# Softplus in the first stage of a one-core layer chain: the rounding rest used as it is, the bias as a ninth product row, maximum and subtraction in one VectorE operation

## The reference, cut to what matters

```
x_dbl = einsum('ble,er->blr', u2, W_xp)
dt_lo, Bm, Cm = x_dbl[..., :8], x_dbl[..., 8:24], x_dbl[..., 24:]
dt = softplus(einsum('blr,re->ble', dt_lo, W_dt) + b_dt)
A = -exp(A_log)
# for each step t:
dA = exp(dt_t[..., None] * A)
h  = dA * h + (dt_t * u_t)[..., None] * Bm_t[:, None, :]
y_t = einsum('ben,bn->be', h, Cm_t)
```

## Time and profile before

| | |
|---|---|
| median of 3 runs | 1540.54 us (1540.09 to 1544.02) |
| span of the profiled execution, its own time | 1563.6 us |
| busy, share of the span: PE, DVE, ACT, POOL | 80%, 65%, 51%, 44% |
| mean granted TensorE clock | 0.902 |
| first work of the four `dt` tiles to the first scan | 35.55 us to 73.71 us |
| loop of the first stage, POOL from first to last product | 73.87 us to 264.13 us |

### The profile page before, as it was taken

One profiled execution on the slowest core, in us unless ns is written; L12 is line 12 of the kernel. 1 busy time (PEld: TensorE's weight loads), 2 busy tenths in 40 slices (PEclk: granted clock), 3 DMA queues, 4 the chain that ended last, 5 costly groups with the idle time before them and its releaser, 6 DMA issues.

```text
span 1563.6 us, 27322 instructions
## 1 busy us (share of the span) xinstructions
PE 1245.3 (80%) x10088; PEld 884.4 (57%) x10088; DVE 1019.5 (65%) x1934; ACT 793.7 (51%) x1635; POOL 694.3 (44%) x688
## 2 busy tenths in 40 slices
PE   6788988224775667878878669988998999986996
PEld 2477877213453324444457424455776777875996
DVE  6898988751111988888663544457976785643774
ACT  4788686102333347767842325546665555321442
POOL 1199987574665430000023310025870881044553
PEclk9689999556888769999989789999999999987998
DMA  6378692112232432211001232111000003001113
GB/s 224 133 279 305 216 365 79 42 48 66 80 84 78 167 104 62 65 59 37 10 27 30 84 128 66 39 57 42 1 1 1 1 1 162 1 26 50 48 46 99
DMA packets 75508, 133.48 MB, mean 85 GB/s; under 512 B 12771, under 2 KB 39846, under 8 KB 74736
## 3 DMA queue, kind: packets, MB, share of 16 engines
q1 hardware_dynamic: 66448, 115.45, 22.0%
q0 software_dynamic: 8064, 13.87, 2.8%
q10 hardware_dynamic: 864, 2.43, 0.4%
HBM read 95.70 MB, written 38.38 MB: 86 GB/s over the span
## 4 chain that ended last, share of the span: by engine, by line
PE 49%; issue 19%; DVE 12%; ACT 8%; DMA 3%; SPq 3%; POOL 3%; another core or an unknown queue 2%; DVEq 0%; POOLq 0%; ACTq 0%
PE ps L1958 5%; PE ps L4214 3%; DVE sb_arena L2024 3%; PE ps L2325 2%; PE ps L718 2%; ACT sb_arena L2272 2%; POOL sb_arena L1116 2%; PE ps L2308 2%; PE ps L2575 1%; PE ps L3295 1%; PE ps L676 1%; PE ps L4181 1%; PE ps L4182 1%; PE ps L4183 1%
## 5 line engine op out<-in xcount | busy, mean ns | idle before, releaser
L2024 DVE TENSOR_REDUCE sb_arena<-ps 128x2 f32<-128x1024 f32 (+2 forms) x192 | 211.2, 1131 | 54.1 <-PE ps L2561 32.5
L2272 ACT ACTIVATE sb_arena<-ps 128x512 f32<-128x512 f32 (+1 forms) x320 | 160.3, 554 | 52.3 <-PE ps L2325 48.4
L921 DVE TENSOR_TENSOR_SCAN sb_arena<-ps,sb_arena 128x1024 f32<-128x1024 f32 x64 | 144.1, 2279 | 17.0 <-ACT ps L1018 16.1
L2056 POOL CAST sb_arena<-sb_arena 128x8 bf16<-128x8 f32 (+2 forms) x32 | 6.5, 204 | 284.0 <-DVE sb_arena L2024 145.4
L1958 PE MATMUL ps<-sb_arena 128*32 128x256 f32 (+3 forms) x1856 | 113.0, 350 | 0.4 <-ACT sb_arena L2514 0.2
L1684 POOL DMA_INDIRECT y<-sb_arena x80 | 77.7, 972 | 54.3 <-ACT sb_arena L1633 33.9
L1116 POOL TENSOR_TENSOR sb_arena<-sb_Wreg,sb_arena 128x1024 f32<-128x1024 f32 x32 | 75.2, 2382 | 54.2 <-DMA sb_arena<-bcrows 45.8
L1217 POOL DMA_INDIRECT xe<-sb_arena x80 | 79.0, 988 | 43.6 <-issue 28.4
L718 PE MATMUL ps<-sb_const,sb_arena 128*128 128x128 f32 x768 | 92.8, 278 | 0.0
L718 PEld LDWEIGHTS ps<-sb_const,sb_arena 128*128 128x128 f32 x768 | 89.9, 194 | 0.5 <-issue 0.5
L2325 PE MATMUL ps<-sb_arena 51*128 51x256 bf16 (+2 forms) x768 | 59.7, 246 | 28.7 <-ACT sb_arena L2272 28.4
(11 more groups left out here) (526 smaller groups left out, 3485.4 us busy)
## 6 DMA issues: line engine op xcount, KB each, us to landing
sb_arena<-bcrows SPq DMA_DIRECT2D x80, 512.0 KB, 5.8
xe<-sb_one SPq DMA_DIRECT2D x31, 260.0 KB, 5.8
sb_Wreg<-e0w SPq DMA_DIRECT2D x24, 256.0 KB, 7.6
sb_arena<-xe SPq DMA_DIRECT2D x16, 325.0 KB
y<-sb_zero SPq DMA_DIRECT2D x20, 256.0 KB, 6.3
sb_Wreg<-e1w SPq DMA_DIRECT2D x16, 256.0 KB, 2.7
sb_Wreg<-e3gu SPq DMA_DIRECT2D x1, 4096.0 KB, 14.0
sb_arena<-y SPq DMA_DIRECT2D x6, 512.0 KB, 4.8
```

Source lines behind the costliest of these rows:

```text
L921: e.tensor_tensor_scan(self.hh[i % 3], k.pair(2 * (i % 2)).rearrange("p c t -> p (c t)"), self.dB[i % 3], 0.0, MUL, ADD).then_inc(S.scan.s ...
L2024: e.tensor_reduce(dst, src, AX.X, MAX).then_inc(S.mxr.sem, 1)
L2272: e.activation(self.PT[s % 4][:, 2 * h:2 * h + 2, 0:n], bank[:, :, 0:n], ACT.Exp, scale=self.scale).then_inc(S.ex.sem, 1)
```

## The change

1. The bias is no longer added by ACT or DVE. `W_dt` gets it as a ninth row (partition 104), and `bc` is filled with ones on partitions 96 to 104 by a new POOL memset of 9x2048; the copy of the rows overwrites 96 to 103. `project_dt` multiplies nine rows instead of eight.
2. The rest r is subtracted as it is, without the factor 1/u. `inverses_act` (four ACT activations) and the multiplication L840 (four DVE operations) are gone.
3. Maximum and subtraction are one DVE operation for every n, (x max 0) - r, with x in PSUM and r in SBUF. It stands behind `up_dve` of the same n. `relu_act`, the old `relu_dve` and the subtraction L842 are gone; `add_log_dve` becomes the first operation of `sum_dve`.
4. Waits: `project_dt` of n = 2 and 3 waits for the new `relu_dve` of n = 0 and 1 (signal `tm`). `c_rows_pe` waits for `tm` of n = 3; it waited for `abs_act` of n = 3 and `relu_act` of n = 3. The first decays wait for `tm` of n = 2.
5. On ACT the copy of the second sequence's rows (`rows_act`) stands ahead of the first logarithm, not between the two.

```diff
-            t = e.matmul(..., wdt[96:104, eb, :], self.bc[96:104, b, c * 512:(c + 1) * 512], start=True, stop=True)
+            t = e.matmul(..., wdt[96:105, eb, :], self.bc[96:105, b, c * 512:(c + 1) * 512], start=True, stop=True)
...
     def c_rows_pe(self, e, w):
-        w.wait_ge(S.sabs, 4)
-        w.wait_ge(S.tma, 2)
+        w.wait_ge(S.tm, 4)
...
-    def add_log_dve(self, e, w, n):
...
-        w.mark(e.tensor_tensor(dt, dt, self.l_[b][eb], ADD))
+    def relu_dve(self, e, w, n, pair):
+        w.wait_ge(S.tq, n + 1)
+        e.scalar_tensor_tensor(self.two(self.dt[b][:, eb, :]), k.pair(2 * pair), 0.0, self.two(self.ex[b][eb]), MAX, SUB).then_inc(S.tm.sem, 1)

     def sum_dve(self, e, w, n):
-        w.wait_ge(S.tr, n + 1)
-        w.wait_ge(S.tq, n + 1)
-        w.mark(e.tensor_tensor(self.ex[b][eb], self.ex[b][eb], self.u_[b][eb], MUL))
-        w.own()
-        e.tensor_tensor(dt, dt, self.ex[b][eb], SUB).then_inc(S.dt.sem, 1)
+        w.wait_ge(S.tm, n + 1)
+        w.wait_ge(S.ln, n + 1)
+        e.tensor_tensor(dt, dt, self.l_[b][eb], ADD).then_inc(S.dt.sem, 1)
         e.tensor_tensor(self.du[b][:, eb, :], dt, self.u2[b][:, eb, :], MUL).then_inc(S.du.sem, 1)
...
# DVE's list
-        self.relu_dve(e, w, 0, 1)
-        self.relu_dve(e, w, 1, 2)
-        self.up_dve(e, w, 0)
-        self.up_dve(e, w, 1)
-        self.add_log_dve(e, w, 0)
-        self.add_log_dve(e, w, 1)
-        self.sum_dve(e, w, 0)
-        self.sum_dve(e, w, 1)
...
+        for b in range(2):
+            for eb in range(2):
+                self.up_dve(e, w, 2 * b + eb)
+                self.relu_dve(e, w, 2 * b + eb, 1 + eb)
+            self.sum_dve(e, w, 2 * b)
+            self.sum_dve(e, w, 2 * b + 1)
...
# decay
-            w.wait_ge(S.sabs, 4)
-            w.wait_ge(S.tma, 2)
+            w.wait_ge(S.tm, 3)
...
# ACT's list
+        self.rows_act(e, w, 1, 0)
         self.log_act(e, w, 0)
-        self.rows_act(e, w, 1, 0)
         self.log_act(e, w, 1)
-        self.inverses_act(e, w, 0)
         self.copy_z(e, w, 0, 3)
...
-        for n, pair in ((2, 1), (3, 2)):
-            self.abs_act(e, w, n, pair)
-            self.relu_act(e, w, n, pair)
+        self.abs_act(e, w, 2, 1)
+        self.abs_act(e, w, 3, 2)
         self.exps_act(e, w, 1)
         self.copy_z(e, w, 1, 0)
         self.log_act(e, w, 2)
         self.log_act(e, w, 3)
-        self.inverses_act(e, w, 1)
...
# POOL's list
         e.memset(self.eps[:, 1:2], 1e-10).then_inc(S.eps.sem, 1)
+        w.wait_ge(S.eps, 1)
+        e.memset(self.bc[96:105, :, :], 1.0).then_inc(S.ones.sem, 1)
+        w.wait_ge(S.ones, 1)
```

More of the change, by code:

```diff
@@ L19 @@
 BIG = 1.0e30
-PACK = [("ln_g", 1), ("ln_b", 1), ("conv_w", 8), ("conv_b", 2), ("b_dt", 2), ("A_log", 32), ("D_param", 2),
+PACK = [("ln_g", 1), ("ln_b", 1), ("conv_w", 8), ("conv_b", 2), ("A_log", 32), ("D_param", 2),
         ("res", 1), ("W_dt", 256), ("wgT", 32), ("rw1", 8), ("rb1", 8), ("ob1", 4), ("b1", 32), ("qn_s", 8),
@@ L485, in __init__ @@
             ip=4, tap=4, conv=4, u2=4, zp=4, sz=4, zcp=2, xp=2, bc=2, bw=32, cTm=1, cT=1,
-            dtm=4, sabs=4, tm=2, tma=2, ex1=4, up1=4, ln=4, tq=4, tr=4, dt=4, du=4, p1=1, res=16,
+            dtm=4, ones=1, sabs=4, tm=4, ex1=4, up1=4, ln=4, tq=4, dt=4, du=4, p1=1, res=16,
             B0=176, B1=176, B2=192, B3=192, B4=160, B5=160, C0=128, C1=128, hT=96, dA=64, dB=64, scan=64, hcv=16, hca=64, hcp=16, acc=64,
@@ L539, in wait_hc @@
             self.wait_half(w, i, 1)
[L541 to L546, removed]
     def rows_out(self, e, w, b):
@@ L644, in project_dt @@
         for c in range(2):
-            t = e.matmul(k.b(2 * pair + c), wdt[96:104, eb, :], self.bc[96:104, b, c * 512:(c + 1) * 512], start=True, stop=True)
+            t = e.matmul(k.b(2 * pair + c), wdt[96:105, eb, :], self.bc[96:105, b, c * 512:(c + 1) * 512], start=True, stop=True)
         t.then_inc(S.dtm.sem, 1)
@@ L814, in conv_dve @@
         e.scalar_tensor_tensor(dst[:, 3:1024], u[:, 0:1021], cw[:, eb, 0:1], dst[:, 3:1024], MUL, ADD).then_inc(S.conv.sem, 1)
[L816 to L819, removed]
     def up_dve(self, e, w, n):
@@ L826, in up_dve @@
         e.scalar_tensor_tensor(self.ex[b][eb], self.u_[b][eb], 1.0, self.ex[b][eb], SUB, SUB).then_inc(S.tq.sem, 1)
-    def add_log_dve(self, e, w, n):
[L829 to L832, removed]
-        w.mark(e.tensor_tensor(dt, dt, self.l_[b][eb], ADD))
+    def relu_dve(self, e, w, n, pair):
+        k, S, b, eb = self.k, self.S, n // 2, n % 2
+        w.wait_ge(S.tq, n + 1)
+        e.scalar_tensor_tensor(self.two(self.dt[b][:, eb, :]), k.pair(2 * pair), 0.0, self.two(self.ex[b][eb]), MAX, SUB).then_inc(S.tm.sem, 1)
     def sum_dve(self, e, w, n):
@@ L967, in late_silu_z @@
         e.activation(z, z, ACT.Silu).then_inc(S.sz.sem, 1)
[L969 to L972, removed]
     def silu_z(self, e, w, n, pair):
@@ L986, in abs_act @@
         w.wait_ge(S.dtm, n + 1)
-        e.activation(self.two(self.ex[b][eb]), k.pair(2 * pair), ACT.Abs, bias=k.s("b_dt")[:, eb:eb + 1]).then_inc(S.sabs.sem, 1)
+        e.activation(self.two(self.ex[b][eb]), k.pair(2 * pair), ACT.Abs).then_inc(S.sabs.sem, 1)
     def exps_act(self, e, w, b):
@@ L999, in log_act @@
         e.activation(self.l_[b][eb], self.u_[b][eb], ACT.Ln).then_inc(S.ln.sem, 1)
[L1001 to L1007, removed]
     def decay(self, e, w, i):
@@ L4614, in lay_out @@
         "conv_w": d["L0_attn_conv_w"].reshape(2, 128, 4).transpose(1, 0, 2).reshape(128, 8),
-        "conv_b": cols(d["L0_attn_conv_b"], 2), "b_dt": cols(d["L0_attn_b_dt"], 2),
+        "conv_b": cols(d["L0_attn_conv_b"], 2),
         "A_log": d["L0_attn_A_log"].reshape(2, 128, 16).transpose(1, 0, 2).reshape(128, 32),
         "D_param": cols(d["L0_attn_D_param"], 2), "res": rows(d["L0_attn_res_scale"]),
-        "W_dt": np.tile(d["L0_attn_W_dt"], (16, 1)), "wgT": d["L0_ffn_wg"].T, "rw1": d["L1_ffn_router_w"],
+        "W_dt": np.concatenate([np.tile(d["L0_attn_W_dt"], (13, 1)), rows(d["L0_attn_b_dt"])[0:24]], axis=0), "wgT": d["L0_ffn_wg"].T, "rw1": d["L1_ffn_router_w"],
         "rb1": rows(d["L1_ffn_router_b"]), "ob1": cols(d["L1_ffn_ob1"], 4),
```

## The result

The changed kernel is slower. Over 20 runs of each it takes 1549.45 us in the median (1541.39 to 1555.56) against 1544.18 us (1538.70 to 1550.12), a ratio of 1.0033 with a 95% interval of 1.0020 to 1.0047, so 3 to 7 us. Single runs spread by 11 to 14 us, far more than the three shown with the kernel before. Those three were also low for it: their median was 1540.54 us, 3.6 us under that of the 20, and the forecast of 1539.7 us is built on them.

What follows compares the result with a forecast made beforehand. The prediction took POOL to bound the first stage's loop: the last `du` 4.8 us earlier, of which the late `c_rows_pe` left 0.8, so 1540.5 - 0.8 = 1539.7 us. Its range of 8 in 10 was 1535.7 to 1542.3 us.

Steps and rivals of the forecast that it cites:

- the last `du`: DVE result that lets POOL enter the first stage's loop; forecast at 69.0 us against 73.8, 4.8 us earlier.
- The block by POOL's first product: `dB` of item 0 on POOL holds up DVE's `up_dve` n = 3 by 1.1 us, bounds 0 and 2.35.
- rival D: ACT or PE late elsewhere, such as a sixth table load of 1.28 us; 1539.7 to 1541 us, chance 0.03.
- The way through `cT`: Second way into the loop: `c_rows_pe`, copy to `cT`, `turn_h`, `times_dve`, scan 2; scan 2 forecast at 79.95, before 79.63.
- I take all of it at the lower level: 2 x 5.87 = 11.7 us: PE's `c_rows_pe`, starting at 64.35 after 6 us of idle, was to end at 76.1.
- my own sum: Chain from `c_rows_pe` to POOL's fifth product: scan 2 at 79.95, its end at 82.25, fifth product at 82.3.
- 1.2 us of slack: POOL's fifth product starts at 83.1, scan 2 ends at 81.9; 0.8 of 4.8 us gained were to pass through.
- (B): `c_rows_pe` runs at 2.4 GHz in part (1537.4 us) or in whole (1535.8 us); chance 0.20.
- (C): DVE loses a whole POOL product or two blocks before relu n = 3; 1.2 us slower, 1541.7; chance 0.12.
- Theory 1: Theory of the experiments: the loss is `c_rows_pe`, moved behind the last relu where TensorE idled and is slow, delaying everything behind `cT`.

Runs made afterwards that it cites:

- e8: Kernel before with only the bias as ninth row and the memset of ones, no bias in L819, L972, L987; ratio to before 0.9985 (0.9963 to 1.0007).
- e11: The changed kernel as it is, traced a third time; no device time or ratio is given.
- e2: Changed kernel with the two bank pairs exchanged, so `c_rows_pe` waits for relu n = 2; ratio to before 0.9962 (0.9940 to 0.9985).
- e1: Changed kernel with the products of `start_y` done three times more, keeping TensorE busy before `c_rows_pe`; ratio to before 0.9991 (0.9968 to 1.0014).
- e6: Changed kernel with bank pairs exchanged as in e2, and the products of `start_y` done once more; ratio to before 0.9966 (0.9947 to 0.9985).
- e3: Kernel before with one wait more: `c_rows_pe` also waits for the last of the four inverses; ratio to before 1.0015 (0.9988 to 1.0042).
- e7: Changed kernel with only the first half of `c_rows_pe` (32 of 64 products), output not the reference's; ratio to before 0.9980 (0.9961 to 0.9999).
- e5: The changed kernel as it is, on the chip of e6 to e8; ratio to before 1.0026 (1.0008 to 1.0045).
- e4: Kernel before with only the four inverses and four products L840 removed, the rest subtracted as it is; ratio to before 0.9963 (0.9940 to 0.9986).

## Why the prediction was wrong

The forecast was 0.8 us faster; measured are 3 to 7 us slower. (1549.45 us also lies 9.7 us above the forecast's 1539.7, but 3.6 of these are the low median of three runs that it starts from, and say nothing of the change.)

**Up to the last `du` the steps held.** The new relu took 1.22 us, nearer to L856 than the 1.28 I took. Relu n = 3 ended at 63.6 (64.2 forecast), the last `du` at 68.4 (69.0). The block by POOL's first product fell on `up_dve` n = 3 as said, 0.9 us (1.58 against 0.69) for my 1.1. The relu beside it, with one input in PSUM, was not blocked. The memset (1.80 us) and the ninth row cost nothing (e8), and no sixth table load came, so rival D is out.

**The way through `cT` was seen, and its length mis-sized.** The step that failed first is "I take all of it at the lower level: 2 x 5.87 = 11.7 us". All of it was at the lower level, but that costs 14.0 us. 5.87 us is the second half's time in a trace in which the clock fell only after that half had begun: the row of 61 to 65 says 0.72, not 0.50. Cut finer, the same trace has 1.00 up to 62, 0.87 in 62 to 63 and 0.50 from there. I took the 0.50 of the idle stretch behind it for its clock. With 14.0 us my own sum gives scan 2 at 82.2 instead of 79.95; it was 81.41, mostly because relu n = 3 was 0.6 us early. By that sum scan 2 ends, and POOL's fifth product starts, at 84.5 instead of 83.1, and the change already loses there.

**The second step that failed** is that POOL "has 1.2 us of slack, so of 4.8 us 0.8 are left" and that these pass through because the loop is POOL's. In all traces of the table the end lies 181.8 to 182.8 us behind scan 2. Behind POOL's fifth product it lies 178.5 to 179.5 us where POOL ran on up to it, and 179.4 to 180.1 us where it had paused. In the changed kernel the fifth product was 0.8 to 1.0 us later than before and the end 1.3 us on average (0.9 to 1.8). The waits view has POOL waiting on scans later in the loop, in before (us in total, times, longest) and for the same 4.2 us on read-outs in the changed kernel:

```profile
POOL sb_arena L1128 <- DVE sb_arena L921: 4.2, 2, 2.5
POOL sb_arena L1116 <- DVE sb_arena L921: 2.5, 3, 1.0
```

And the chain that ended last, in the trace of before, is PE's in the very stretch in which POOL has no pause:

```profile
82.28 2.06 PE ps L676 x8
84.33 4.73 PE ps L718 x32
89.06 0.87 PE ps L676 x8
89.93 1.79 PE ps L718 x16
```

Added up between 80 and 262 us it lies on PE for 88 us, on POOL for 34, on ACT for 22 and on DVE for 19. So a busy 125.13 of 126 us in the earlier trace rows showed that POOL had no pause in that stretch; it didn't make POOL the only bound of the loop, which goes on to 264 us. As an estimate: with scan 2 at my own 79.95, 0.3 us later than before, and the end bound to scan 2 within the 1.0 us above, there was no gain to be had.

**The rivals.** (B) did not come: behind 5.3 us of idle PE both halves ran at 0.50. It was closer than the prediction had it, for in the changed kernel's trace the clock was still 1.00 for most of the idle stretch and fell 0.3 us before the block:

```profile
58.50:63.40 4.90, 0.00 (x0) 0.00 (x0) 4.83 (x4) 4.31 (x4) 2.03 (x1) 1.00 1.03 384
63.40:63.66 0.26, 0.01 (x1) 0.01 (x1) 0.26 (x2) 0.25 (x2) 0.00 (x0) 0.53 1.16 221
```

In e11 it fell between 60.0 and 60.5 us, and in e2 within the half microsecond in which the block starts (0.95 in 57.0 to 57.5, 0.50 behind it). e1 and e6 show what it would have given: from a busy TensorE the first half is fast and the second is not, and most of the gain comes. The rule that (B) cites from the Trainium skill, TensorE: Matmul & The Clock Gate, part 1, that sustained activity lifts the clock, isn't borne out for these products here: the clock fell under them in e1 and e6 with PE busy, and did not rise in the changed kernel's 14 us of them. (C) named the right sign and a wrong cause: the block on DVE was shorter than forecast. That the sign of a rival came out is luck. I had bound the slower side by POOL's product alone and given `c_rows_pe` no bound above 11.7 us, though the trace had no row of it wholly at 0.50.

**Theory 1 is shown up to the end of the first stage's loop.** e3 delays `c_rows_pe` alone and moves the end; e1 and e7 shorten it alone, by clock and by count, and the end comes back; e2 and e6 move the wait and turn the loss into a gain, in device time too.

**Open.** The stage explains 2.5 us, inside the 1.3 to 7.1 us of e5 and a little under the 3.1 to 7.3 us of the 20 runs. Only 1.3 of the 2.5 lie before the end of the loop, where theory 1 is shown. Another 0.3 us lie between there and the last 32 products: 13.4 us from the mark "end" to their start in all seven traces built on the changed lists, e6 and e7 included, and 13.0 to 13.1 in the six built on those of before. In the seven, DVE stands idle before its last product with the gate (`gate_dve`, L846, L863 before) for a reason that the profile doesn't show:

```profile
273.45 1.22 DVE L846 TENSOR_TENSOR sb_arena<-sb_arena,ps 128x1024 f32<-128x1024 f32 x1 [0.26 <-issue]
```

In the six it follows without a gap. This part isn't `c_rows_pe`, and its cause is open. The last 0.8 us lie in the stage's last 32 products, 6.2 to 6.4 us in three traces of the changed kernel and 5.2 to 5.6 in three of before; but they take 6.0 and 6.1 us in e4 and e8, which are not slower, and 6.6 in e1. Why they take longer in the changed kernel was not found. The anchor also leaves something out: it came between 40.6 and 43.1 us, and late in two traces of each kind (before and e4, changed and e11), in which the first eight products of the x projection took 5.35 us instead of 3.65. Nor was it tried whether more is lost in the later layers: single runs spread too far.

## What to carry to other kernels

When a change shortens the work ahead of a loop, look for whatever it moves **behind** that work: here one wait of a small block of products, harmless with 7 us to spare, took the whole gain and more. Price a TensorE block that now starts behind an idle stretch by rows that lie wholly at the lower clock, and check that level over the row's own time. If there is none, take twice the full-clock time as the bound of your estimate (here 7.0 us against 3.64). And take the bound of a loop from its whole length and from the chain that ended last: an engine that is busy all through the first part can wait in the second, and another chain can pass on a loss at the start. Last, take the base of a forecast from enough runs: three of them lay 3.6 us too low here.

## What the runs showed of the hardware

In these traces the 128x16 products with 128x128 weights took 3.64 us for 32 at clock 1.00 (the 2.4 GHz level) and 7.0 us at 0.50 (the 1.2 GHz level). The clock fell under them: in e1 it was 1.00 up to 65 us with PE busy 3.86 to 4.00 of 4.00 us, and then 0.54

```profile
61.00:65.00 4.00, 3.86 (x33) 3.58 (x33) 3.93 (x5) 2.40 (x3) 0.00 (x0) 1.00 0.89 363
65.00:69.00 4.00, 4.00 (x22) 4.00 (x22) 3.67 (x3) 0.00 (x0) 2.77 (x2) 0.54 0.34 139
```

with PE busy for all of it. So here the busy share of PE did not tell what the clock would do. And one more round of `start_y`'s products (2.87 us in its row), put where PE would have stood idle for 2.19 us, made the 32 products behind it 3.3 us faster, 3.64 against 6.98 us (e6 against e2).
